# Cross-attention's value sums moved by DMA into one row per channel, instead of transposes on TensorE

## The reference

```python
x = _layernorm(x + _L0_attn_ref(x, L0_attn_w_project, L0_attn_w_out), axis=-1)
x = _layernorm(x + _L0_xattn_ref(x, ctx_2048, ...), axis=-1)
x = _layernorm(x + _L0_ffn_ref(x, ...), axis=-1)
```

```python
q = split_heads(_proj(x, Wq, bq)); k = split_heads(_proj(c, Wk, bk)); v = split_heads(_proj(c, Wv, bv))
q = _apply_rotary(q_emb, q);       k = _apply_rotary(k_emb, k)
scores = jnp.einsum('bhtc,bhsc->bhts', q, k) / math.sqrt(K_CH)
p_attn = jax.nn.softmax(scores, axis=-1)                     # over 256 keys s
out = jnp.einsum('bhts,bhsc->bhtc', p_attn, v)               # 8 channels a head
return _proj(out.transpose(0, 1, 3, 2).reshape(b, 64, t_t), Wo, bo)
```

## Time and profile before

| | |
|---|---|
| median of 3 runs (lowest, highest) | 564.52 us (564.18, 565.63) |
| profiled execution: its time, its span | 564.45 us, 562.4 us |
| PE, DVE, ACT, POOL busy | 80%, 79%, 68%, 51% of the span |
| first block | from the start to about 421 us |
| one body in the steady part (bodies 1 to 12) | 22.8 us |

### The profile page before, as it was taken

How to read it: one execution, slowest core, us unless ns; L and a number is a source line. 1 busy time by engine, 2 the same in 40 slices (tenths; PEclk the granted TensorE clock), 3 DMA queues, 4 the chain that set the end, 5 groups by cost and what they waited for, 6 DMA issues and landing times. The chain is left out here.

```text
span 562.4 us, 11994 instructions
## 1 busy us (share of the span) xinstructions
PE 449.5 (80%) x4145; PEld 241.7 (43%) x4162; DVE 443.6 (79%) x965; ACT 381.8 (68%) x698; POOL 289.3 (51%) x387
## 2 busy tenths in 40 slices
PE   6567899999999999999999999889987701555563
PEld 5343544545555455554554544433333200333342
DVE  3747587888978979889798897876747959999973
ACT  2222366767667667676686766777676887999972
POOL 5753564447455574464654745530031827667652
PEclk9778799999999999999999999995797975555555
DMA  6143318223232232332422323120000000000010
GB/s 217 48 127 119 115 37 259 62 75 100 54 105 67 64 109 61 90 84 56 108 70 72 104 53 94 50 68 9 2 2 1 0 1 1 10 28 19 30 37 29
DMA packets 51674, 37.07 MB, mean 66 GB/s; under 512 B 21408, under 2 KB 47648, under 8 KB 51488
## 3 DMA queue, kind: packets, MB, share of 16 engines
q1 hardware_dynamic: 51328, 36.10, 22.6%
q10 hardware_dynamic: 288, 0.23, 0.2%
HBM read 24.52 MB, written 10.49 MB: 62 GB/s over the span
## 5 line engine op out<-in xcount | busy, mean ns | idle before, releaser
L968 DVE TENSOR_REDUCE MX<-mx_b 128x2 f32<-128x512 f32 x256 | 167.9, 679 | 38.1 <-PE mx_b L579 36.8
L773 ACT ACTIVATE PB<-e_b 128x512 f32<-128x512 f32 x256 | 149.5, 592 | 68.0 <-PE e_b L607 67.1
L579 PE MATMUL mx_b<-KA,QA 48*128 48x256 bf16 x512 | 101.5, 284 | 9.1 <-DVE MX L968 8.7
L607 PE MATMUL e_b<-QA,KA 50*128 50x256 bf16 x512 | 101.4, 283 | 3.0 <-ACT PB L773 2.1
L624 PE MATMUL u_b<-PB,VA 128*32 128x256 f32 x1024 | 87.1, 406 | 3.8 <-ACT PB L773 3.3
L895 POOL TENSOR_TENSOR SP<-SP,srec 128x1024 f32<-128x1024 f32 x15 | 28.5, 1901 | 82.0 <-DVE srec L940 82.0
L579 PEld LDWEIGHTS mx_b<-KA,QA 48*128 48x128 bf16 x512 | 30.4, 95 | 87.5 <-issue 48.3
L1233 POOL TENSOR_TENSOR H<-H,row_tab 128x1024 f32<-128x1024 f32 x16 | 37.7, 2357 | 23.0 <-ACT H L1191 19.5
L1280 PE MATMUL r_b<-identh,Q 128*128 128x128 f16 x128 | 16.6, 311 | 39.5 <-ACT Q L1201 39.5
L1286 PE MATMUL z_b<-w2q,Q2T 128*128 128x256 bf16 x128 | 30.2, 418 | 19.3 <-ACT Q2T L1212 19.3
L314 POOL TENSOR_TENSOR rs<-mv,epsc 128x1 f32<-128x1 f32 x32 | 6.1, 189 | 72.9 <-DVE mv L301 50.0
(11 more groups left out here) (169 smaller groups left out, 1044.2 us busy)
## 6 DMA issues: line engine op xcount, KB each, us to landing
KA<-parts_k SPq DMA_DIRECT2D x64, 96.0 KB
QA<-parts_q SPq DMA_DIRECT2D x64, 96.0 KB
parts_q<-part_q SPq DMA_DIRECT2D x32, 128.0 KB, 2.1
parts_k<-part_k SPq DMA_DIRECT2D x16, 192.0 KB, 2.1
C<-in_ctx SPq DMA_DIRECT2D x16, 128.0 KB, 3.0
X<-in_x SPq DMA_DIRECT2D x16, 128.0 KB, 2.9
out_y<-O SPq DMA_DIRECT2D x16, 128.0 KB, 1.7
XT<-in_xT SPq DMA_DIRECT2D x15, 128.0 KB, 2.1
```

What stands on the lines that cost most here:

```text
L579: m = nc.tensor.matmul(mx_b[n % 2][:, D * k:D * k + D], QA[low:low + K_MAX, 2 * i.ring + b, h, P * u:P * u + P], KA[low:low + K_MAX, 2 * i ...
L607: m = nc.tensor.matmul(e_b[n % 2][:, D * k:D * k + D], KA[low:low + K_EXP, 2 * i.ring + b, h, P * sc:P * sc + P], QA[low:low + K_EXP, 2 * ...
L773: nc.scalar.activation(PB[:, n % 4].rearrange("p e t -> p (e t)"), e_b[n % 2][:, :], ACT.Exp, scale=XC ** -0.5).then_inc(e_sb.sem, 1)
L968: nc.vector.tensor_reduce(MX[:, b, e, 2 * q:2 * q + 2, u], mx_b[n % 2][:, :].rearrange("p (e s) -> p e s", e=2), AXL.X, ALU.max).then_inc( ...
```

## The change

What it does:

- US is no longer transposed. SP issues eight DMAs for each half (`realign`): four copy the 8 channel rows of a group of 32 to 16 rows of 256 in UV, four copy 8 of the rows that hold the sum to the same rows of RB. The result has a row for each channel, and the sum of the weights beside it eight times over.
- One DVE reciprocal of 128x256 for a whole pair (`reciprocals`, slot 3 of the next body, where `u_norm(prev, 1)` stood) and one POOL product (`means`) write AT. `u_transpose`, `att_transpose`, `u_norm` and `at_copy` are gone.
- V's bias goes into the output bias once (`value_bias`: one matmul, one DVE add); Wo's columns are permuted on the host to the new row order.
- In `scores`, the two mask products take 64 rows each, for the two banks, with an identity folded to half its rows.
- In the second block the end of the last pair moves a few turns later: `reciprocals` in turn 2, `x_out_proj` in turn 6, `norm2` in turn 8, `factors` in turn 13.

```diff
+        def realign(sp, i, b):
+            if b == 0 and has(i, 1):
+                wait(sp, at_sb, i.plus(-1), 1)
+            wait(sp, u_sb, i, b + 1)
+            for j in range(4):
+                for dst, low in ((RB, 32 * j + XC), (UV, 32 * j)):
+                    sp.dma_start(dst[HALF * b + 16 * j:HALF * b + 16 * j + 16, :],
+                                 US[low:low + XC].rearrange("c s t -> c (s t)")).then_inc(moved[b], 16)
+
+        def reciprocals(dve, i):
+            for b in range(2):
+                dve.wait_ge(moved[b], NMOVED * (i.v + 1))
+            nc.vector.reciprocal(RB[:], RB[:]).then_inc(u_rec.sem, 1)
+
+        def means(pool, i):
+            wait(pool, u_rec, i, 1)
...
+            nc.gpsimd.tensor_tensor(AT[:], UV[:], RB[:], ALU.mult).then_inc(at_sb.sem, 1)
@@ SP body @@
+                if real(prev):
+                    realign(sp, prev, 1)
                 if i.v >= 1 and real(a):
                     load_c(a)
+                if real(a):
+                    cross_values(a)
                 if real(i):
                     max_rows(i, 1)
-                if real(a):
-                    cross_values(a)
                 if real(j):
                     store_parts("q", j)
+                if real(i):
+                    realign(sp, i, 0)
                 if real(nxt):
                     max_rows(nxt, 0)
...
             bodies(sp, body)
+            realign(sp, Pair(0, NPAIR - 1), 1)
@@ PE @@
+                banks = [use(g_b[r], sc_sub, a, 4 - r) for r in range(2)]
                 for r in range(2):
-                    ps = use(g_b[r], sc_sub, a, 4 - r)
-                    nc.tensor.matmul(ps[:, :], identb[:], maskb[:].rearrange("p h s -> p (h s)"),
+                    rows = slice(HALF * r, HALF * r + HALF)
+                    nc.tensor.matmul(banks[r][:, :], identb[rows, :], maskb[rows].rearrange("p h s -> p (h s)"),
                                      start=True, stop=False, skip_group_check=True)
...
-                    if s == 3 and real(prev):
-                        u_transpose(pe, prev, 1, use(g_b[2], u_nrm, prev, 4))
-                    if s == 5 and real(prev):
-                        att_transpose(pe, prev, use(g_b[2], at_sb, prev, 1))
-                    if s == 13 and real(i):
-                        u_transpose(pe, i, 0, use(g_b[1], u_nrm, i, 2))
@@ ACT @@
             def u_copy(i, b):
                 wait(act, pv, i, 4 * b + 4)
                 if b == 1:
-                    wait(act, ut_ps, i, 1)
+                    act.wait_ge(moved[0], NMOVED * (i.v + 1))
                 elif has(i, 1):
-                    wait(act, ut_ps, i.plus(-1), 2)
+                    act.wait_ge(moved[1], NMOVED * i.v)
...
-                    if s == 5 and real(prev):
-                        at_copy(act, prev, 2)
@@ DVE @@
                     if s == 3 and real(prev):
-                        u_norm(dve, prev, 1, 2)
+                        reciprocals(dve, prev)
...
-                    if s == 13 and real(i):
-                        u_norm(dve, i, 0, 1)
@@ POOL @@
                     split_parts(pool, nc.gpsimd, "q", j)
+                if real(prev):
+                    means(pool, prev)
                 if real(a):
                     self_norm(pool, nc.gpsimd, a)
```

More of the change, by code:

```diff
@@ L128, in build_layer @@
         US = sb("US", [P, 2, D])
-        RD = sb("RD", [P, 16])
-        AN = sb("AN", [P, 2, 2, SEQ])
+        UV, RB = sb("UV", [P, D]), sb("RB", [P, D])
         AT = sb("AT", [P, D])
+        xbo = sb("xbo", [P, 1])
         Y2, st2, mv2, rs2 = sb("Y2", [P, D]), sb("st2", [P, 6]), sb("mv2", [P, 2]), sb("rs2", [P, 3])
@@ L136, in build_layer @@
         ln1 = event("ln1", 7)
-        u_sb, ut_ps, u_nrm = event("u_sb", 2), event("ut_ps", 2), event("u_nrm", 4)
-        at_ps, at_sb, xo_ps = event("at_ps"), event("at_sb"), event("xo_ps")
+        u_sb, u_rec = event("u_sb", 2), event("u_rec")
+        at_sb, xo_ps = event("at_sb"), event("xo_ps")
+        s_bias_ps, s_bias = sem("s_bias_ps"), sem("s_bias")
+        moved = [sem(f"moved{b}") for b in range(2)]
+        NMOVED = 16 * 8
         ln2 = event("ln2", 7)
@@ L238, in tile_at @@
             return i.plus(n // 16), n % 16
[L241 to L255, removed]
         def x_out_proj(pe, i, ps):
@@ L259, in x_out_proj @@
             nc.tensor.matmul(ps[:, 0:D], xw["o"], AT[:, :], start=True, stop=True).then_inc(xo_ps.sem, 1)
[L261 to L266, removed]
         def square_sum(act, i):
@@ L274, in square_sum @@
                                  accum_out=sumsq[:, bass.ds(i.v, 1)]).then_inc(s_sq, 1)
[L276 to L289, removed]
+        def realign(sp, i, b):
[12 more added lines that the diff above has]
+            wait(pool, u_rec, i, 1)
+            for b in range(2):
+                pool.wait_ge(moved[b], NMOVED * (i.v + 1))
+            if has(i, 1):
+                wait(pool, xo_ps, i.plus(-1), 1)
+            nc.gpsimd.tensor_tensor(AT[:], UV[:], RB[:], ALU.mult).then_inc(at_sb.sem, 1)
         def norm2_stats(dve, i, g):
@@ L294, in norm2_stats @@
                 wait(dve, ln2, i.plus(-1), 7)
+            else:
+                dve.wait_ge(s_bias, 1)
             wait(dve, ln1, i, 7)
-            nc.vector.scalar_tensor_tensor(out=Y2[:].unsqueeze(1), in0=g_b[g][:, 0:D].unsqueeze(1), scalar=xb["o"],
+            nc.vector.scalar_tensor_tensor(out=Y2[:].unsqueeze(1), in0=g_b[g][:, 0:D].unsqueeze(1), scalar=xbo[:],
                                            in1=XALL[:, bass.ds(i.v, 1), :], op0=ALU.add, op1=ALU.add).then_inc(ln2.sem, 1)
@@ L627, in pv_quad, with value_bias @@
                 last.then_inc(pv.sem, 1)
+            def value_bias(g):
+                ps = use(g_b[g], Event(s_bias, 0), Pair(0, 0), 1)
+                pe.wait_ge(ld_cross, NCROSS)
+                nc.tensor.matmul(ps[:, 0:1], xw["o"], xb["v"], start=True, stop=True).then_inc(s_bias_ps, 1)
             def weight_total(g):
@@ L677, in body @@
                         transpose_p(a)
-                    if s == 13 and real(i):
-                        u_transpose(pe, i, 0, use(g_b[1], u_nrm, i, 2))
+                    if s == 11 and i.v == 0:
+                        value_bias(1)
                     if s == 13 and real(a):
@@ L985, in weight_clip, with value_bias @@
                     nc.vector.tensor_scalar(q[:].rearrange("p k n -> p (k n)"), w[:], -1.0, None, ALU.max).then_inc(s_wclip[k], 1)
+            def value_bias():
+                dve.wait_ge(s_bias_ps, 1)
+                nc.vector.tensor_tensor(xbo[:], g_b[1][:, 0:1], xb["o"], ALU.add).then_inc(s_bias, 1)
             def weight_scale():
@@ L1024, in body @@
                         norm2_stats(dve, prev, 1)
-                    if s == 13 and real(i):
-                        u_norm(dve, i, 0, 1)
+                    if s == 11 and i.v == 0:
+                        value_bias()
                     if s == 14 and real(prev):
@@ L1216, in _ @@
                 first_values(t)
-                if t == 1:
-                    at_copy(act, last, 0)
-                if t == 5:
+                if t == 8:
                     norm2(act, last)
@@ L1246, in _ @@
             mean_power(pool, 1)
+            means(pool, last)
             rstd(pool, ln2, last, mv2, rs2)
-            mean_power(pool, 2)
             for n in range(NPAIR):
+                if n == 5:
+                    mean_power(pool, 2)
                 wait(pool, qb, Pair(0, n), 1)
@@ L1289, in _ @@
             pe.wait_ge(s_tab, 3)
-            u_transpose(pe, last, 1, g_b[1])
             for t in range(TURNS1):
-                if t == 2:
-                    att_transpose(pe, last, g_b[0])
-                if t == 3:
+                if t == 6:
                     x_out_proj(pe, last, g_b[1])
@@ L1382, in _ @@
             for t in range(TURNS1):
-                if t == 1:
-                    u_norm(dve, last, 1, 1)
+                if t == 2:
+                    reciprocals(dve, last)
                 if t == 4:
-                    norm2_stats(dve, last, 1)
                     factors(dve, 1)
                 if t == 7:
+                    norm2_stats(dve, last, 1)
+                if t == 10:
                     norm2_max(dve, last)
@@ L1394, in _ @@
                     first_bias(i)
-                if t == 9:
+                if t == 13:
                     factors(dve, 2)
```

11 lines of the change are left out of this document (7 added, 4 removed).

## The result

| | before | after |
|---|---|---|
| median (lowest, highest), 4 runs each | 564.96 us (564.18, 565.63) | 720.73 us (720.28, 721.92) |
| ratio, 95% interval | | 1.277 [1.274, 1.280] |
| span of the profiled execution | 562.4 us | 718.5 us |
| mean distance of two C loads, body 1 to body 12 | 23.08 us | 33.44 us |

The direction and the mechanism were as forecast. The size was not: 661 us was named, with 708 us as the upper end, and the kernel takes 13 us more than that end.

What follows compares the result with a forecast made beforehand. PE bounds the kernel before, DVE close behind; after the change, a loop through SP's copies, DVE and SP's next body. 564.45 + 81.6 + 2 + 3 + 5.9 + 4 = 661 us; range 622 to 708 us.

Steps and rivals of the forecast that it cites:

- The loop: From SP's first copy to the next body's: copies and landing 5.7, reciprocal 1.7, return 20.6, sum 28.0 us for 22.8.
- PE's savings: On PE, fewer transposes and one mask step less: 1.7 us a body, not on the loop and bringing nothing.
- The landing: On SP's copies: data land 2.2 us from issue, as VM<-VS has it.
- the slope of the earlier trace: On DVE: 6.0 ns an element, from reciprocals of 16 and 2 elements a row, giving 1.7 us for 128x256.
- I take 0.50 us, eight in 4.0 us: On SP: the step from one copy's issue to the next is 0.50 us, bounded by 0.43 and 0.67 us.
- the return way of 20.6 us: From slot 4's maximum tile to SP's next C load: 21.36 us less DVE's 0.73 us wait for scores, 20.6 us.
- predicted at 1.6 from the half clock of the earlier trace: On PE behind its stop of about 5.5 us: the lower clock lengthens a body by another 1.6 us.
- the 29.6 us predicted: Likeliest steady body with the lower clock behind PE's stop: 29.6 us, 6.8 us more than before.
- 5.9 + 0 + 4 = 9.9 us: End of the first block: body 13 +5.9 us, bodies 14 and 15 0, last eight copies before the barrier +4 us.
- SP is free, the wait is short: In bodies 14 and 15: PE's 1.7 us a body pay for the short wait, 0 us (-4 to +4).
- 81.6 + 3 us: Twelve loops, body 1 to body 13, at 6.8 us each, and +3 us for body 1's shared DMA engines.
- the clock stays low for most of a body: Rival on PE's clock: 34 us or so a body, 12 x 11 = 134, about 710 us; chance 0.12.

Runs made afterwards that it cites:

- the full clock that won next to nothing: Changed kernel with 36 unread matmuls behind slot 5 and 5 behind slot 6 of each body: 729.21 us, a body of 32.88 us.
- the two remedies together: Changed kernel with four DMAs a pair in place of sixteen copies and their result used a body later: 559.18 us, 162 us won.
- the fourth kernel: Change with four DMAs a pair through HBM, used a body later, loads moved behind the query store: 559.18 us, ratio 0.989 to the kernel before.
- the table of four kernels: Complete change with sixteen copies, used next body 720.73 us or a body later 665.62 us; with four DMAs, 663.62 us or 559.18 us.
- the kernel with four DMAs used early: Change with four DMAs a pair through HBM in place of sixteen copies, used in the next body: 663.62 us, a body of 29.40 us.

## Why the prediction was right, and where it failed

**Right, with its rows.** The loop exists: SP's copies come straight behind KA's expansions, DVE waits in slot 3 for a DMA of UV in 15 bodies, PE has one long gap a body, the clock falls to 0.50 in the steady part, and the second block keeps its length. PE's savings bring nothing, since they are not on the loop; a body 1.2 us shorter than before was seen only where nothing waits. The landing, 2.1 us for a predicted 2.2 us, and the reciprocal, 1.75 us for 1.7 us, were right, so the slope of the earlier trace rows holds within 5% out to 256 elements.

**The step that failed: "I take 0.50 us, eight in 4.0 us".** It is 0.73 us, above my upper bound of 0.67 us. The reason given for the value was that the rows are as plain as C's and the ends as small as MR's. The earlier trace rows held the better neighbour, VM<-VS, which is what the copies are: from SBUF to SBUF. I took it only as a bound because its pieces are small. The error is 7 x 0.23 = 1.6 us a body; first issue to DVE's start was 7.2 us for 5.7 us.

**The second failed step: the return way of 20.6 us, counted on one way only.** The term was "from the maximum tile of slot 4 to SP's next C load". In the body read above it is 329.91 - 306.14 = 23.8 us. Of the 3.2 us, 2.5 are the clock (12.38 us from the row maxima to POOL's variance for 9.85 us), predicted at 1.6 from the half clock of the earlier trace rows; 0.7 are the landing of the key store (3.0 us for 2.4 us) and SP's arrival at it. The sum 7.2 + 1.7 + 23.8 = 32.7 us stands against the 29.6 us predicted; the mean over all loops is 33.4 us. That half 0's copies also stand ahead of that store was written nowhere in the prediction: it costed the sixteen issues, followed the first eight to their waits, and let the other eight go. That SP's list binds as well is shown by the full clock that won next to nothing, and by the two remedies together. The landing of the store grew wherever it stands right behind the queries' expansions and the X load (3.0 us here, 3.4 us at 323.69 with the clock held); where SP's list has 2.4 us to spare, as without half 0's copies or with four DMAs, it is 2.4 us again. So the 0.7 us come with the same overlooked group; what makes them there was not tested.

**The ends.** Body 13 to the barrier was costed at 5.9 + 0 + 4 = 9.9 us and took 26.5 us. In bodies 14 and 15 "SP is free, the wait is short" was wrong:

```profile
557.51 1.75 DVE L271 RECIPROCAL RB<-RB 128x256 f32<-128x256 f32 x1 [5.28 <-DMA UV<-US]
```

Half 1 reaches US only in slot 0, and seven steps and a landing from there are 7.2 us even on a free SP: ACT's copy to US ends at 550.28, and 550.28 + 7.2 = 557.5. The last eight copies, from 571.41 to 577.2, cost 5.8 us ahead of the barrier, predicted 4. Body 0 was costed at 2 us and took 5.0 us. Body 1 was costed at 3 us more than a usual loop; its distance of C loads is 36.06 us, 2.6 us above the mean, where before had 24.33 us, 1.3 us above it.

**In sum:** the twelve loops 125.5 us in place of 81.6 + 3 us, the end of the block 26.5 us in place of 9.9 us, the start 5.0 us in place of 2 us. Of the rivals, "the clock stays low for most of a body" gave 34 us a body and 710 us, close to the number by a mechanism that is not the one at work: the clock was back after 8 us of 33, and held at full it gives 0.6 us. With the stop itself the low clock lasts 13.7 us, still less than half of a body. That this rival came near the number was luck. The upper end of 708 us is no sum of terms: both upper bounds together give a loop of 29.7 us, with the clock 31.3 us, and 564.45 + 12 x 8.5 + 15 = 681 us; the rest was margin, and no case in it had the second group of copies on a path.

**Few DMAs for many.** The number of DMAs shows in the issuing queue: sixteen issues of 16 KB take 16 x 0.725 = 11.6 us of SP in each body, the four larger ones of the fourth kernel 2 x 0.33 + 0.65 + 0.62 = 1.9 us, and with the use a body later the same layout goes from 27.7% slower to 1.1% faster.

## What to carry to other kernels

Before a step is given to a queue that issues in order, count its instructions, take the step from the trace's nearest transfer with the same ends (SBUF to SBUF here), and walk every instruction behind each group to the engine that needs it; a list that had 2.2 us to spare does not take 5.8 us more. Where several waits lie over each other, removing one shows little: both have to go, as the table of four kernels shows. A long operation on an engine that another follows closely belongs where that engine has slack: two slots were worth some 29 us.

## What the runs showed of the hardware

- A copy of 16 rows of 1 KB from SBUF to SBUF holds SP for 0.68 us, with a step of 0.73 us to the next, while C's load of 128 rows of 1 KB holds it for 0.39 us and, in the kernel with four DMAs used early, UV's load of 128 rows from HBM for 0.60 us; QA<-MR, 4 KB, holds it for half of 1.16 us. The cost of these issues does not follow their bytes.
- Two stops of PE as short as 0.51 and 1.42 us, close together, were followed by a granted clock of 0.50 for 3.4 us, body after body (the kernel without copies). In the kernel before, the longest gap for DVE there is 0.36 us, and the clock is 1.00 from 100 to 353 us.
- The reciprocal of 128x256 takes 1.75 us, (1752 - 165) / 254 = 6.2 ns an element above a row of 2, where an ordinary pass of that size takes 0.41 us.

```profile
L271 DVE RECIPROCAL RB<-RB 128x256 f32<-128x256 f32 x16 | 28.0, 1752 | 108.9 <-DMA UV<-US 108.9
```
